# A one-core recommendation tower: first-cycle order, layer two in halves, and compares against numbers kept in PSUM

## The reference

```python
e = jnp.stack([tbl_0[ids[:, 0]], ..., tbl_25[ids[:, 25]]], axis=1)      # 2048 x 26 x 128
T = jnp.concatenate([r_dense[:, None, :], e], axis=1)                   # 27 vectors
Z = jnp.einsum('bnd,bmd->bnm', T, T)
z = Z[:, iu0, iu1]                                                      # upper triangle, k=1: 351 pairs
h = jnp.concatenate([z, r_dense], axis=1)
h = jnp.maximum(h @ W_top1 + b_top1, 0.0)                               # 479 -> 512
h = jnp.maximum(h @ W_top2 + b_top2, 0.0)                               # 512 -> 256
y = h @ W_top3                                                          # 256 -> 1
```

## Time and profile before

| | us |
|---|---|
| three runs | 357.80, 357.87, 363.47 (median 357.87) |
| profiled execution, device time | 359.46 |
| its span, first to last instruction | 357.6 |

### The profile page before, as it was taken

How to read it: one execution, slowest core, us unless ns; L and a number is a source line. 1 busy time by engine, 2 the same in 40 slices (tenths; PEclk the granted TensorE clock), 3 DMA queues, 4 the chain that set the end, 5 groups by cost and what they waited for, 6 DMA issues and landing times.

```text
span 357.6 us, 9909 instructions
## 1 busy us (share of the span) xinstructions
PE 342.6 (96%) x4044; PEld 319.0 (89%) x4044; DVE 217.1 (61%) x805; ACT 172.5 (48%) x220; POOL 251.1 (70%) x263
## 2 busy tenths in 40 slices
PE   3998899899999999999999999999999999999997
PEld 1898798889999999989999999999999899988896
DVE  3779969778546655667448484647457575434121
ACT  4668635452475146461474435562463615354511
POOL 6777777777777777777777777777777777777000
PEclk9999999999999999999999999999999999999999
DMA  7997243355325622255223631255222532263330
GB/s 204 258 259 218 67 137 76 94 150 141 131 61 130 179 55 58 56 134 175 53 60 93 148 122 50 64 135 176 55 59 66 144 78 54 67 150 80 69 47 17
DMA packets 45878, 39.07 MB, mean 109 GB/s; under 512 B 32930, under 2 KB 39113, under 8 KB 45834
## 3 DMA queue, kind: packets, MB, share of 16 engines
q1 hardware_dynamic: 36014, 21.40, 22.5%
q0 software_dynamic: 8192, 16.79, 18.8%
q10 hardware_dynamic: 1628, 0.25, 0.5%
HBM read 32.40 MB, written 6.02 MB: 107 GB/s over the span
## 4 chain that ended last, share of the span: by engine, by line
PE 89%; DVE 5%; ACT 2%; DMA 2%; issue 1%; SPq 1%; DVEq 0%
PE look_ps L758 39%; PE gram_ps L785 15%; PE mlp_ps L805 13%; PE look_ps L768 7%; PE mlp_ps L815 7%; PE look_ps L749 4%; DVE hot L458 4%; DMA w<-in_tbl_dram 2%; ACT T L616 1%; PE look_ps L826 1%; PE look_ps L848 1%; DVE tab_lo L444 1%; ACT T L604 1%; PE gram_ps L826 0%; PE mlp_ps L826 0%
## 5 line engine op out<-in xcount | busy, mean ns | idle before, releaser
L427 POOL DMA_INDIRECT rows<-in_tbl_dram,ids_all x240 | 234.1, 976 | 73.2 <-issue 71.6
L458 DVE TENSOR_SCALAR hot<-ids_near 125x256 fp32r<-125x256 f16 x640 | 150.0, 305 | 61.1 <-PE look_ps L758 53.5
L758 PE MATMUL look_ps<-hot,tab_hi 125*128 125x256 f32 x616 | 153.6, 290 | 2.4 <-DVE hot L458 1.2
L758 PE MATMUL look_ps<-hot,tab_lo 125*128 125x256 f32 x616 | 149.2, 283 | 0.0
L758 PEld LDWEIGHTS look_ps<-hot,tab_hi 125*128 125x128 f32 x616 | 117.6, 191 | 5.0 <-issue 1.4
L758 PEld LDWEIGHTS look_ps<-hot,tab_lo 125*128 125x128 f32 x616 | 117.8, 191 | 0.1
L616 ACT COPY T<-look_ps 128x384 f32<-128x384 f32 (+1 forms) x80 | 79.0, 1095 | 21.4 <-PE look_ps L768 21.4
L608 ACT COPY T<-look_ps 128x512 f32<-128x512 f32 x32 | 38.4, 1200 | 96.7 <-PE look_ps L758 56.4
L785 PEld LDWEIGHTS gram_ps<-T 128*54 128x54 f32 x2048 | 54.0, 130 | 9.3 <-ACT T L616 2.5
L785 PE MATMUL gram_ps<-T 128*54 128x54 f32 x2048 | 58.0, 214 | 3.4 <-DVE gram L482 1.6
L482 DVE COPY gram<-gram_ps 128x486 f32<-128x486 f32 (+1 forms) x64 | 37.3, 601 | 14.5 <-PE gram_ps L785 12.6
(11 more groups left out here) (72 smaller groups left out, 137.9 us busy)
## 6 DMA issues: line engine op xcount, KB each, us to landing
dots<-gram SPq DMA_DIRECT2D x28, 182.2 KB
ids_near<-ids_rows SPq DMA_DIRECT2D x7, 640.0 KB
rows<-in_tbl_dram,ids_all POOLq DMA_INDIRECT x240, 2.6
T<-in_tbl_dram SPq DMA_DIRECT2D x4, 448.0 KB
pairs<-dots SPq DMA_DIRECT2D x14, 117.0 KB
gram<-in_tbl_dram SPq DMA_DIRECT2D x3, 448.0 KB
rows<-in_r_dense_dram SPq DMA_DIRECT2D x16, 64.0 KB, 3.8
pairs<-dots SPq DMA_DIRECT2D x7, 104.0 KB
```

Of the source, the lines that this page charges most:

```text
L427: pool.indirect_dma_start(rows[:, t % 2, place[n], :], None, tables[n - 1], bass.IndirectOffsetOnAxis(ap=index[:, n - 1:n].bitcast(U32), a ...
L458: eq = nc.vector.tensor_scalar(hot[:VP, at % 2, c], ids_near[:VP, u % 2, k], float(c), None, ALU.is_equal)
L758: mm = pe.matmul(dst, w[:VP, k, c], hot[:VP, slot, c], start=(c == 0 and half == 0), stop=(c == CH - 1 and half == 1))
```

## The change

1. DVE, unit 0 and unit 1: of the four block copies of tile 0, two now come before `compare(1, 1)` and two behind; the split of table 1 moves from behind `compare(1, 5)` to behind those copies; `compare(1, 6)` comes ahead of `dense_out(0, 1)`; two block copies of tile 1 come ahead of `compare(1, 7)` and two behind.
2. PE, each cycle: the half of `layer2` for the first tile goes between the third and the fourth round of turns, the other half stays at the end. In the last stage `layer1(END - 1, 12, 16)` comes whole behind the last turn.
3. DVE, from unit 3 on: compares at all places but 3 and 9 are one TENSOR_TENSOR of 125 x 2048 elements, `ids_near` (repeated over chunks) against the chunk numbers 0 to 7, which lie in eight words of the second `gram_ps` bank and are written once by eight memsets. Since PE writes that bank in blocks 1 and 3, waits on `hot_ready` and one on `steps_ready` keep PE out of it while such a compare reads it.

```diff
--- before.py
+++ after.py
@@ -94,7 +94,7 @@
     VP = V // CH
     VP16 = VP // 16 * 16
     assert VP * CH == V and VP <= P and V <= 2048 and D == P and F1C == 4 and F2C == 2 and K % 2 == 0
-    assert NV % 2 == 1 and MC * PC == NV and KP <= P and 18 * NV <= 512 and dense_round == NR - 1
+    assert NV % 2 == 1 and MC * PC == NV and KP <= P and 18 * NV <= 500 and dense_round == NR - 1
     w1_pieces = pair_weight_pieces(NV, HALF, MC)
     STORED = 16 * NJ
     SHUFFLED = 16 * (PC + 1)
@@ -153,6 +153,9 @@
         look_ps = psum("look_ps", [P, RING, 512], F32)
         gram_ps = psum("gram_ps", [P, 2, 512], F32)
         mlp_ps = psum("mlp_ps", [P, 2, 2, Q], F32)
+
+
+        steps = gram_ps[:, 1, 500:500 + CH]
 
         ids_first_landed = sem("ids_first_landed")
         ids_landed = sem("ids_landed")
@@ -183,6 +186,7 @@
         turned = sem("turned")
         look_free = sem("look_free")
         dense_ready = sem("dense_ready")
+        steps_ready = sem("steps_ready")
         gram_done = sem("gram_done")
         gram_free = sem("gram_free")
         l1_done = sem("l1_done")
@@ -207,6 +211,11 @@
 
         def looks(u):
             return LOOKS if u else LOOKS_FIRST
+
+        def by_steps(u, at):
+
+
+            return u >= 3 and at not in (3, 9)
 
         looked_first = [k for g in LOOKS_FIRST for k in g]
         looked = [k for g in LOOKS for k in g]
@@ -454,9 +463,16 @@
                     dve.wait_ge(ids_relative, K * (u + 1))
                 if K * u + at >= 2:
                     dve.wait_ge(hot_looked, K * u + at - 1)
-                for c in range(CH):
-                    eq = nc.vector.tensor_scalar(hot[:VP, at % 2, c], ids_near[:VP, u % 2, k], float(c), None,
-                                                 ALU.is_equal)
+                if by_steps(u, at):
+                    if u == 3 and at == 0:
+                        dve.wait_ge(steps_ready, CH)
+                    near = ids_near[:VP, u % 2, k:k + 1].to_broadcast([VP, CH, Q])
+                    eq = nc.vector.tensor_tensor(hot[:VP, at % 2], near, steps[:VP].rearrange(
+                        "p (c q) -> p c q", q=1).to_broadcast([VP, CH, Q]), ALU.is_equal)
+                else:
+                    for c in range(CH):
+                        eq = nc.vector.tensor_scalar(hot[:VP, at % 2, c], ids_near[:VP, u % 2, k], float(c), None,
+                                                     ALU.is_equal)
                 eq.then_inc(hot_ready, 1)
 
             def dense_out(u, l):
@@ -528,17 +544,22 @@
                 if at > 6:
                     split(looked_first[at])
                 compare(0, at)
+
+            dve.wait_ge(ids_t_ready, UNITS)
+            for c in range(CH):
+                nc.vector.memset(steps[:, c:c + 1], float(c)).then_inc(steps_ready, 1)
             compare(1, 0)
             dense_out(0, 0)
+            gram_out(0, 0, (0, 1))
             compare(1, 1)
-            gram_out(0, 0)
-            for at in range(2, 6):
+            gram_out(0, 0, (2, 3))
+            split(WHOLE[0])
+            for at in range(2, 7):
                 compare(1, at)
-            split(WHOLE[0])
             dense_out(0, 1)
-            compare(1, 6)
+            gram_out(0, 1, (0, 1))
             compare(1, 7)
-            gram_out(0, 1)
+            gram_out(0, 1, (2, 3))
             split(WHOLE[1])
             compare(1, 8)
             split(WHOLE[2])
@@ -777,6 +798,11 @@
                         pe.wait_ge(look_free, use_of["look", u, len(looks(u)) - 1] + 1)
                 if BLOCKS * t + b >= 2:
                     pe.wait_ge(gram_free, BLOCKS * t + b - 1)
+
+                if t == 0 and b == 0:
+                    pe.wait_ge(steps_ready, CH)
+                if b % 2 == 1 and 1 < u < END:
+                    pe.wait_ge(hot_ready, K * (u + 1) + (2 if l == 0 else 8) + (b == 3 and (l == 0 or u + 1 < END)))
                 src = T_tile(u, l).rearrange("p (g i s) n -> p g i (s n)", g=2, s=2)
                 first, end = pieces(u, l)[b]
                 for i in range(first, end):
@@ -807,14 +833,15 @@
                     if c == PC and f % 2 == 1:
                         mm.then_inc(l1_done, 1)
 
-            def layer2(u):
+            def layer2(u, tiles=range(2)):
 
                 pe.wait_ge(h1_ready, F1C * (u + 1))
-                for l in range(2):
+                for l in tiles:
                     for c in range(F1C):
                         mm = pe.matmul(mlp_ps[:, 0, l], h1[:, c, l * P:(l + 1) * P], w2[:, c],
                                        start=(c == 0), stop=(c == F1C - 1))
-                mm.then_inc(l2_done, 1)
+                if l == 1:
+                    mm.then_inc(l2_done, 1)
 
             def last_layer1(l):
                 def product(f, c, first):
@@ -935,9 +962,12 @@
                     look(u + 1, 3)
                 look(u + 1, 4)
                 look(u + 1, 5)
-                for r in range(NR):
+                for r in range(3):
                     turn(u + 1, 0, r)
-                layer2(u - 1)
+                layer2(u - 1, [0])
+                for r in range(3, NR):
+                    turn(u + 1, 0, r)
+                layer2(u - 1, [1])
             turn(END, 1, 0)
             for b in range(BLOCKS):
                 products(END, 0, b)
@@ -946,10 +976,9 @@
             turn(END, 1, 2)
             layer1(END - 1, 8, 12)
             turn(END, 1, 3)
-            layer1(END - 1, 12, 14)
             turn(END, 1, 4)
 
-            layer1(END - 1, 14, 16)
+            layer1(END - 1, 12, 16)
             for b in range(BLOCKS):
                 products(END, 1, b)
             layer2(END - 1)
```

## The result

Fourteen runs of each: median 356.51 us against 358.27. Every ratio in this document leaves out executions more than 1.5% above the fastest of their kernel (here three of the changed kernel, 359.87 to 360.31 us); this one is 0.9925, 95% interval 0.9902 to 0.9948, some 2.7 us faster. The forecast was 356.6 (355.1 to 358.2), 1.3 us faster. The profiled execution of the changed kernel takes 355.16 us with a span of 353.3; that of before took 359.46 and 357.6.

What follows compares the result with a forecast made beforehand. PE's own stream was taken to bound the kernel, with idle time mostly in the first cycle. Terms -1.0 - 0.6 - 0.1 + 0.4 = -1.3 us took the median 357.87 to 356.6 us, range 355.1 to 358.2.

Steps and rivals of the forecast that it cites:

- First cycle, -1.0: DVE reordering in the first cycle lets PE go on earlier: -1.0 us, bounds -0.3 and -2.0.
- no split and no `dense_out` stands ahead of compare (1, 6): First cycle on DVE: with these moved away, PE's 1.60 us wait ahead of tile 1's block 2 is gone.
- The two copies of tile 0: First cycle on DVE: taking two ahead of compare (1, 1) gives PE's block 2 at most 0.1 us, taken as 0.
- PE's late signal: First cycle: gain only 0.3 us if PE's signals come as late as the 0.76 us ahead of 45.34 at more places.
- Memsets, 0.5 us and hidden: Eight memsets ahead of compare (1, 0) on DVE: 0 to 1.3 us, taken as 0.5, hidden, so 0 in the sum.
- Layer two in halves, -0.6: Half of layer two ahead of round 3 covers the late turns' waits for PSUM banks: -0.6 us, bounds -0.7 and 0.
- The end: Last stage: `layer1(12, 16)` whole behind the last turn covers its copy better, -0.1 us (0 to -0.15).
- The compare, 2300 ns: New one-instruction compare on DVE takes 2.30 us, 0.43 more than before; bounds 1.87 and 2.84 us.
- The wait ahead of look 4 of unit 7: Last cycle: PE's wait for place 8's compare grows from 0.26 to 0.7 us, +0.4 us (0 to +1.0).
- The cover of the waits: In the cycles PE reaches block 3 after the compare is done, 0.5 us to spare; added waits taken as 0.
- rival C: New compare much dearer than 2.30 us, for instance 4.4; block 3 waits in nine places, 373 us; chance 0.05.
- Rival B: Last gathered rows land late on POOL, PE waits ahead of the last turn; gain ends at 2.1 us, 355.8; chance 0.04.

Runs made afterwards that it cites:

- e1: Kernel before with only the first cycle's new DVE order (copies and split moved); ratio 0.9998 (0.9967 to 1.003) to the kernel before.
- e5: Kernel before with one edit: two block copies of tile 1 ahead of compare (1, 7), split left in place; one execution, 356.65 us.
- e6: Kernel before with one edit: the split of table 1 moved ahead of compare (1, 2); one execution, 358.64 us.
- e2: Kernel before with only layer two's halves and the last layer-one piece whole behind the last turn; ratio 0.9973 (0.9947 to 0.9998).
- e3: Changed kernel with both reorderings undone, so only the PSUM compares, their memsets and PE's added waits are new; ratio 1.0008 (0.9985 to 1.0032).
- e4: Kernel before with both reorderings (first cycle, layer two's halves) but the old compares; ratio 0.9963 (0.9941 to 0.9986).
- e7: Changed kernel with two more gathers on POOL, into an unused tile; ratio 0.9960 (0.9926 to 0.9995) to the kernel before.
- e8: Changed kernel with PSUM compares from unit 2's place 2, old compare at last unit's place 8, unit 5's `y_out` behind two copies; 354.65 us, ratio 0.9899.

## Why the prediction was right, and where its steps were off

*What bounds it, and the direction.* Right: PE's stream, and the idle time lay in the first cycle and ahead of the turns.

*First cycle, -1.0: the size in its bounds, the cause off.* The stretch is 2.2 us shorter between the two traces, of which the edit gives 1.55 (see e1). The step "no split and no `dense_out` stands ahead of compare (1, 6)" gave the wrong edit the credit: e5 removes the wait with the split in place, e6 keeps 1.23 us of it. Compare (1, 7), 1.87 us, stood between the block and its copy. The two copies of tile 0 were costed at nothing, and that holds: the blocks of tile 1 start 16.8 us behind the first products (59.32 - 42.49) instead of 17.5 (60.32 - 42.81), but e2 and e3, with the old order there, need 16.9 as well. What was wrong there is to take PE's late signal, a copy at 45.34, for a fixed thing: in e3 that copy starts 1.65 us behind the first products, in before 2.53.

*Memsets, 0.5 us and hidden.* Hidden, and they take 0.12 us together.

*Layer two in halves, -0.6: the mechanism right, the size a third.* The bounds were -0.7 and 0. The term counted the idle time in the window, 0.12 us a cycle. A cycle fell by 0.31, five times, and a sixth time in the last cycle (41.48 to 41.55 although its compare took 0.37 more). The transposes behind the wait took 0.52 us instead of 0.33, a slow restart of 0.19 that the profile counts as busy: -1.9 in all, outside the bounds. e2 has it, e3 has not. The end gave 0.2 instead of 0.1.

*The compare, 2300 ns.* Measured 2286. The wait ahead of look 4 of unit 7 rose from 0.26 to 0.63 us, +0.37 against +0.4. The cover of the waits held: no idle time in the cycles; rival C did not come.

*Sum.* The edits: -1.55 - 1.9 - 0.2 (the end) + 0.4 = -3.25 us. With 0.3 from a start that came earlier and 0.7 from the piece up to tile 1's products, neither of which an edit made, this gives, but for rounding, the 4.3 us between the traces. The runs gained 2.7. So PE's stream lost 3.25 us where 1.3 were forecast, two and a half times as much. That the measured median, 356.51, lies 0.1 us from the forecast of 356.6 is luck: the forecast starts from the 357.87 of the first three runs of before, where fourteen give 358.27, and the median is held up by executions that the prediction did not have in mind (below); without the three left out in the ratio it is 355.64.

*Rival B, 0.04: far too low for what it is worth.* It was weighed with a PE gain of 1.3. It does not happen in the profiled execution of the changed kernel, but with the gain that PE really had, unrelieved gathers cost 2.7 us of waits (e4). Part 3, alone worth nothing (e3: 1.0008), thus is what lets the others count in the traces; the runs, 0.9963 without it and 0.9925 with it, point the same way without settling it. The rule of the Trainium skill that GpSimd contends with a VectorE instruction in a 2-port mode or with two SBUF inputs (GPSIMD Engine Reference, section 8, Key points) agrees with the traces: 0.947 us a gather with the compares against PSUM, and no slower beside such a compare than beside nothing, as the rows in the section on the profile show; 0.971 in e4's trace, where the compares have the old form:

```profile
120.00:320.00 200.00, 152.44 (x157) 1.00 0.36 97
```

Which property of the old form slows the gathers, its mode or that there are eight instructions instead of one, no run separates.

*What stays open.* How much of the 3.25 us the runs lose again, and where. The first products start anywhere from 41.20 to 43.13 us in the ten traces outside the last group. In three of them (e2, e3, e7) one gather took 4 to 5 us. The changed kernel asks for the last rows about 5 us earlier than before and would have to wait for such a gather; e2's and e7's traces show PE waiting for rows and, behind the wait, a granted clock of 0.50. The mean granted clocks on record fit this. Of 53 executions of the kernel before in the groups of e1 to e8, one is below 1.00, and of e3's, with PE's stream as it was, none of 12. Of the kernels with a shorter stream, the changed one has 4 of 14 (357.46 to 360.31 us), e1 3 of 12, e2 5 of 13, e4 4 of 12, e7 2 of 10 and e8 1 of 7, mostly their longest executions. So a shorter stream on PE seems to bring the late rows into play in some executions and not in others. None of these executions of the changed kernel was profiled, so for it this is argued, not shown.

## What to carry to other kernels

When a stream that bounds is made shorter, ask what comes next in line: here the gathers had about 3 us of slack at the last turn, and in the traces an edit that costs VectorE 15 us paid for itself by disturbing GpSimd less. An idle gap on PE costs more than its width, so price a removed wait by the distance between marks on both sides, not by the idle time. Take that distance from more than one trace: 0.7 us of what two traces differed by here was in a piece that no edit had touched to any effect. Of several edits in one stretch, ask for each wait which instruction stands directly between producer and consumer; that one is to be moved.

## What the runs showed of the hardware

- One instruction of 125 x 2048 elements with one input in PSUM that repeats a word took 2286 ns, about what the slope between 256 and 512 plain elements gives (2300); the repeated read cost nothing that shows. A memset of one column in PSUM took 59 ns, eight behind one another 0.12 us.
- A gather beside the old compares took 1.01 us in the mean, beside the new ones 0.94, as much as with DVE idle.
- A gather on POOL, in that trace else up to 1.16 us, took 4.13 us in e3:

```profile
57.37 4.13 POOL L436 DMA_INDIRECT rows<-in_tbl_dram,ids_all  x1 [0.30 <-issue]
```

  and 4.86 in e2 and 4.68 in e7, while SP was issuing a row of transfers (weights, or stores of the dot products). Other traces have the same transfers and no such gather; the cause is open.
- After a wait of 0.12 us for a PSUM bank, the next three transposes took 0.52 us instead of 0.33.
- After PE had waited 1.04 and 2.11 us (e2), the granted clock was 0.50 from 335 to 341 us; after 1.74 us (e7) it was 0.50 from 76 to 78. After 0.90 and 1.81 us in e4 it stayed at 1.00.
- On another chip the changed kernel took 580.16 us (median of twelve) at a mean granted clock of 0.81 to 0.82, with PE busy 70% of the span of its trace.
